# Second attention of a two-layer decoder: heads in pairs on the two halves of TensorE's rows

## The reference

```python
def _L1_attn_ref(x, W_qkv, b_qkv, W_proj, b_proj):
    B, N, C = x.shape                       # 2, 1024, 256
    qkv = x @ W_qkv + b_qkv
    qkv = qkv.reshape(B, N, 3, 16, 16)      # 16 heads of 16 columns
    q, k, v = jnp.transpose(qkv, (2, 0, 3, 1, 4))
    scores = jnp.einsum('bhqd,bhkd->bhqk', q, k) * 16 ** (-0.5)
    attn = jax.nn.softmax(scores, axis=-1)
    out = jnp.einsum('bhqk,bhkd->bhqd', attn, v)
    return jnp.transpose(out, (0, 2, 1, 3)).reshape(B, N, C) @ W_proj + b_proj
```

## Time and profile before

| | us |
|---|---|
| median of 3 runs | 2764.35 (2764.23 to 2765.06) |
| the profiled execution, own time | 2767.74 |
| its span in the trace | 2765.9 |
| second attention's loop | from 1894.0 to 2441.0 of the span |
| busy over the whole span | PE 91%, DVE 62%, ACT 46%, POOL 31% |

### The profile page before, as it was taken

The page is one execution under the profiler, slowest core; times in us unless marked ns, Lnnn a source line. Parts: engine busy times, 40 slices in busy tenths (PEclk is TensorE's granted clock), DMA queues, the critical chain, the costliest instruction groups (busy, mean ns, idle before and its releaser), DMA issues.

```text
span 2765.9 us, 35667 instructions
## 1 busy us (share of the span) xinstructions
PE 2511.4 (91%) x13840; PEld 1727.1 (62%) x13840; DVE 1717.4 (62%) x3089; ACT 1282.2 (46%) x2015; POOL 867.3 (31%) x445
## 2 busy tenths in 40 slices
PE   8999998999999789899999999997999999976663
PEld 7554545744554579788888988994555555544421
DVE  5566655376665446875444344356877777847967
ACT  4555554345555144344444444442666555632342
POOL 4777774366777240102222023010200000004323
PEclk9999999999999899899999999998999999987885
DMA  2000001000000210000000010003333232210000
GB/s 74 12 22 14 12 12 43 12 12 23 12 19 1 69 61 1 31 1 31 31 31 20 12 43 9 1 1 83 74 66 70 62 66 62 47 32 9 1 0 31
DMA packets 49641, 84.23 MB, mean 30 GB/s; under 512 B 9912, under 2 KB 30016, under 8 KB 49472
## 3 DMA queue, kind: packets, MB, share of 16 engines
q1 hardware_dynamic: 49328, 81.88, 11.6%
q10 hardware_dynamic: 144, 0.07, 0.0%
HBM read 37.49 MB, written 2.10 MB: 14 GB/s over the span
## 4 chain that ended last, share of the span: by engine, by line
PE 75%; DVE 16%; ACT 3%; issue 3%; POOL 2%; DMA 1%; SPq 0%; ACTq 0%; DVEq 0%; POOLq 0%
PE PS L85 74%; DVE m_gl L1097 2%; DVE PS L576 2%; DVE a_QS L554 1%; ACT a_P L519 1%; DVE a_nm L568 1%; DVE s_nm L1523 1%; DVE X L271 1%; DVE x_E L1922 1%; DVE x_rd L1906 1%; DVE st_s L232 1%; DVE x_sm L1927 1%; POOL f_H L2128 1%; POOL a_sum L676 1%; ACT a_QS L473 1%
## 5 line engine op out<-in xcount | busy, mean ns | idle before, releaser
L1097 DVE TENSOR_TENSOR m_gl<-m_g,m_gh 128x512 fp32r<-128x512 f32 x288 | 258.1, 902 | 386.4 <-ACT m_g L936 386.4
L676 POOL TENSOR_TENSOR a_sum<-a_sum,a_P 128x1024 f32<-128x1024 f32 x192 | 456.6, 2378 | 128.4 <-ACT a_P L519 118.0
L519 ACT ACTIVATE a_P<-PS 128x512 f32<-128x512 f32 x512 | 290.3, 596 | 354.3 <-PE PS L85 349.5
L933 ACT ACTIVATE m_gh<-PS,cols 128x512 fp32r<-128x512 f32 x288 | 198.5, 689 | 469.6 <-PE PS L85 469.6
L1523 DVE TENSOR_REDUCE s_nm<-PS 128x1 f32<-128x512 f32 x512 | 344.8, 688 | 70.0 <-PE PS L85 67.4
L568 DVE TENSOR_REDUCE a_nm<-PS 128x1 f32<-128x1024 f32 x256 | 300.4, 1216 | 128.2 <-PE PS L85 128.2
L85 PE MATMUL PS<-m_w2h,m_gh 128*128 128x256 f32 x1152 | 324.5, 282 | 18.9 <-DVE m_gl L1097 18.7
L1440 ACT ACTIVATE s_P<-PS 128x1024 f32<-128x1024 f32 x256 | 262.1, 1024 | 165.4 <-PE PS L85 164.8
L85 PE MATMUL PS<-m_w2l,m_gh 128*128 128x256 f32 x1152 | 323.1, 280 | 0.0
L85 PE MATMUL PS<-m_w2h,m_gl 128*128 128x256 f32 x1152 | 323.0, 280 | 0.0
L85 PE MATMUL PS<-a_P,a_V 128*64 128x512 f32 x1024 | 250.9, 612 | 0.0
(11 more groups left out here) (304 smaller groups left out, 4346.8 us busy)
## 6 DMA issues: line engine op xcount, KB each, us to landing
m_raw<-in_m_w SPq DMA_DIRECT2D x16, 1024.0 KB, 5.2
s_Q<-s_T SPq DMA_DIRECT2D x128, 128.0 KB, 2.4
s_K<-s_T SPq DMA_DIRECT2D x128, 128.0 KB, 2.4
a_KH<-a_KH SPq DMA_DIRECT2D x64, 128.0 KB, 2.3
a_wr<-in_w_qk SPq DMA_DIRECT2D x16, 256.0 KB, 2.9
X<-in_x SPq DMA_DIRECT2D x4, 512.0 KB, 6.6
a_P<-in_w_v SPq DMA_DIRECT2D x8, 256.0 KB, 5.8
a_P<-in_w_o SPq DMA_DIRECT2D x2, 1024.0 KB, 5.5
```

Source lines behind the costliest of these rows:

```text
L519: e.activation(a_P[:, g % N_P, half * 512:half * 512 + 512], PS[:, 2 + half, :], ACT.Exp).then_inc(s["a_exp"], 1)
L676: e.tensor_tensor(o[:, :], a_P[:, (g - 1) % N_P, :] if k == 1 else o[:, :], a_P[:, g % N_P, :], ALU.add).then_inc(s["a_add"], 1)
L933: e.activation(m_gh[r][:, :], PS[:, 4 + n % 3, :], func, bias=cols[:, bcol:bcol + 1]).then_inc(s["m_gh"], 1)
L1097: e.tensor_tensor(m_gl[r][:, :], m_g0[r][:, :], m_gh[r][:, :].bitcast(F32), ALU.subtract).then_inc(s["m_gl"], 1)
```

## The change

Heads go in pairs (`p`, 16 of them; two halves `q` of 512 queries in each). Each head of a pair has 64 partitions of `s_Q` and `s_K` (`R[0]` and `R[1]`): 32 for high times high with the maximum's row, 16 for low times high, 16 for high times low. Low times low is left out, and so is the maximum's low part (`s_ml`), since a shift that is the same everywhere cancels in the softmax. `R_S` is 3. There are 256 steps again, with as many matmuls of each kind; each of the natural and transposed ones now contracts over 64 partitions.

- natural: 128 queries by 512 keys of both heads, into bank pair 0, 1 or 2, 3; one DVE reduce over 1024 columns a step.
- transposed: 128 keys by 512 queries of both heads, head a into bank 4 + a. Each has its own exponential of 512 columns; the next matmul into that bank waits for it.
- values: two steps' worth together, in every second step. Bank 6 is copied once, by ACT, into `s_zt`, and SP moves it to `s_Z` with two DMAs.
- the gather is 12 DMAs for each pair, issued at step 16k + 15; the maxima's row goes in two DMAs for each half pair.
- `turned` for the first four tiles moves into the loop, the first projections use four banks, and transposed matmuls stand at a step's start.

```diff
-        R_S = 4
+        R_S = 3
-        s_P = [sb(c, f"s_P{i}", [128, S]) for i in range(3)]
+        s_P = [sb(c, f"s_P{i}", [128, S]) for i in range(4)]
+            if x in (228, 236, 244, 252):
+                side[x].append(("turned", (x - 228) // 8))
...
             for x in range(N_X):
-                if x < 8 * NH:
-                    natural(x, 0)
-                extra = list(side[x])
-                if extra and extra[0][0] == "rows":
-                    piece(extra.pop(0))
                 w = x - LAG_S
-                if 0 <= w < 8 * NH:
-                    h, kt = divmod(w, 8)
-                    bk = (2, 4)[w % 2]
+                if 0 <= w < N_U:
+                    p, half, kt = w // 16, (w // 8) % 2, w % 8
                     if kt == 0:
-                        e.wait_ge(s[f"row{h % 2}"], 256 + 32 * (h // 2 + 1))
-                    if w >= 2:
-                        e.wait_ge(s["s_exp"], w - 1)
-                    for half in range(2):
-                        t = mm(e, PS[:, bk + half, :], Ks[h % R_S][:, kt * 128:(kt + 1) * 128],
-                               Qs[h % R_S][:, half * 512:half * 512 + 512], True, True)
-                    t.then_inc(s["s_st"], 1)
-                if x < 8 * NH:
-                    natural(x, 1)
+                        e.wait_ge(s[f"row{(w // 8) % 2}"], 256 + 32 * (w // 16 + 1))
+                    for a in range(2):
+                        if w:
+                            e.wait_ge(s["s_exp"], 2 * w + a - 1)
...
+                        mm(e, PS[:, 4 + a, :], Ks[p % R_S][R[a], kt * 128:(kt + 1) * 128],
+                           Qs[p % R_S][R[a], half * 512:half * 512 + 512], True, True).then_inc(s["s_st"], 1)
+                if x < N_U:
+                    p, i, half = x // 16, (x // 2) % 8, x % 2
...
+                    for a in range(2):
+                        t = mm(e, PS[:, 2 * half + a, :], Qs[p % R_S][R[a], i * 128:(i + 1) * 128],
+                               Ks[p % R_S][R[a], half * 512:half * 512 + 512], True, True)
+                    t.then_inc(s["s_n"], 1)
                 y = x - LAG_P
-                if 0 <= y < 8 * NH:
...
+                if y % 2 and 0 < y < N_U:
+                    for y in (y - 1, y):
...
+                        for c in range(4):
+                            part = 512 * (c % 2) + 256 * (c // 2)
+                            t = mm(e, PS[32 * c:32 * c + 32, 6, 0:256], V1[:, kt, (h + c % 2) % 16, :],
+                                   s_P[y % 4][:, part:part + 256], kt == 0, kt == 7)
...
-                    e.activation(s_P[w % 3][:, :].rearrange("p (a n) -> p a n", a=2), PS[:, bk:bk + 2, :],
-                                 ACT.Exp, scale=0.25).then_inc(s["s_exp"], 1)
+                    for a in range(2):
+                        e.wait_ge(s["s_st"], 2 * w + a + 1)
+                        e.activation(s_P[w % 4][:, a * 512:a * 512 + 512], PS[:, 4 + a, :],
+                                     ACT.Exp, scale=0.25).then_inc(s["s_exp"], 1)
...
+                    e.tensor_reduce(nm2[:, p % 2, :, i, half], PS[:, 2 * half:2 * half + 2, :], AX.X, ALU.max,
+                                    negate=True).then_inc(s["s_nr"], 1)
...
         def sp_l1a(e):
-            def gather(h):
+            def gather(p):
+                g = p // 2
...
+                    e.wait_ge(s["s_b7"], n_b7["proj", g, 3])
+                if p >= R_S:
+                    e.wait_ge(s["s_st"], 32 * (p - R_S) + 32)
...
+                for what in side[x]:
+                    if what[0] == "rows":
...
+                        e.wait_ge(s["s_mhd"], q + 1)
...
-                if 0 <= w < 8 * NH and w % 8 == 7 and w // 8 + R_S < NH:
-                    gather(w // 8 + R_S)
+                if x >= 15 and x % 16 == 15 and x // 16 + 2 < N_PR:
+                    gather(x // 16 + 2)
```

More of the change, by code:

```diff
@@ L1227, in program @@
         for x in range(N_X):
-            if 0 <= x - LAG_M < 8 * NH and (x - LAG_M) % 8 == 0:
-                side[x].append(("rows", (x - LAG_M) // 8))
+            if x >= 9 and (x - 9) % 8 == 0 and (x - 9) // 8 < 2 * N_PR:
+                side[x].append(("rows", (x - 9) // 8))
             y = x - LAG_P
-            if 0 <= y < 8 * NH:
-                if y // 8 == 15:
-                    side[x].append(("values", y % 8))
-                if y % 32 == 31:
-                    pb, pg = y // 128, (y // 32) % 4
-                    todo += [("sums", pb, pg), ("spread", pb, pg), ("scale", pb, pg, 0), ("scale", pb, pg, 1)]
-                    if pg == 3:
-                        for q in range(2):
-                            todo += [("project", 8 * pb + j) for j in range(4 * q, 4 * q + 4)]
-                            todo.append(("norm", 8 * pb + 4 * q))
@@ L1241, in program @@
-            if todo and x // 8 % 4 > 1 and x % 8 in (3, 5, 7):
+            if y % 2 == 1 and 120 <= y < 128:
+                side[x] += [("values", y - 121), ("values", y - 120)]
+            if 0 <= y < N_U and y % 32 == 31:
+                pb, pg = y // 128, (y // 32) % 4
+                todo += [("sums", pb, pg), ("spread", pb, pg), ("scale", pb, pg, 0), ("scale", pb, pg, 1)]
+                if pg == 3:
+                    for q in range(2):
+                        todo += [("project", 8 * pb + j) for j in range(4 * q, 4 * q + 4)]
+                        todo.append(("norm", 8 * pb + 4 * q))
@@ L1251, in program @@
-        before = {7: len(i7), 6: None}
-        for i, what in enumerate(rest):
-            if what[0] not in ("spread", "norm"):
-                bank7[what], i7_free[what] = 7 - i % 2, before[7 - i % 2]
-                i7[what] = before[7 - i % 2] = len(i7) + 1
+                who = {"rows": "s_mhd", "turned": "t_xl"}.get(what[0], "s_b7")
+                count[who] += 1
+                i7_free[what], bank7[what], n_b7[what] = last_b7[bk], bk, count[who]
+                if what[0] != "turned":
+                    i7[what] = len(i7) + 1
@@ L1449, in act_l1a @@
-                for what in extra:
-                    if what[0] == "spread":
+                    if q >= 2:
+                        e.wait_ge(s[f"s_zd{q % 2}"], 32 * (q // 2))
+                    e.activation(s_zt[:, q % 2, :], PS[:, 6, 0:256], ACT.Copy).then_inc(s["s_za"], 1)
+                for what in side[x]:
+                    if what[0] == "rows":
+                        q = what[1]
+                        e.wait_ge(s["s_p7"], i7[what])
+                        if q >= 2:
+                            e.wait_ge(s[f"row{q % 2}"], 256 + 32 * (q // 2))
+                        e.activation(s_mh[:, q % 2, :], PS[0:8, 7, 0:128], ACT.Copy).then_inc(s["s_mhd"], 1)
+                    elif what[0] == "spread":
@@ L1533, in piece @@
                     tiles = range(what[1], what[1] + 4)
-                    slow.append(norm_steps(e, own, tiles, {j: (s["s_b7"], i7["project", j]) for j in tiles}))
+                    slow.append(norm_steps(e, own, tiles, {j: (s["s_b7"], n_b7["project", j]) for j in tiles}))
+                elif what[0] == "turned":
+                    late.append(what)
                 elif what[0] == "proj":
                     late.append(what)
-                elif what[0] != "spread":
+                elif what[0] not in ("spread", "rows"):
                     bk = bank7[what]
@@ L1559, in dve_l1a @@
                     slow.append(round_steps(e, own, range(6)))
-                if x < 8 * NH:
-                    natural(x, 0)
-                if late:
-                    _, g, u = late.pop()
-                    low(g, u, 7).then_inc(s["s_b7"], 1)
-                extra = list(side[x])
-                if extra and extra[0][0] == "rows":
-                    _, h = extra.pop(0)
-                    e.wait_ge(s["s_mhd"], h + 1)
-                    e.tensor_tensor(s_ml[:, h % 2, :], PS[0:8, 7, 0:128], s_mh[:, h % 2, :].bitcast(F32),
-                                    ALU.subtract).then_inc(s["s_b7"], 1)
@@ L1589, in dve_l1a @@
             pump(slow, 99)
-            for i in range(4):
-                turned(i, i % 2)
             for what in rest:
```

278 lines of the change are left out of this document (125 added, 153 removed).

## The result

The changed kernel takes 2794.6 us as a median of four runs (2788.3 to 2800.5). The kernel before took 2764.3 beside it, so the ratio is 1.0111, with an interval of [1.0088, 1.0134]: 1.1% slower, some 30 us. The forecast was 2771.

A forecast was written before the change was run, and what follows sets the result against it. PE was taken to bound the loop, busy 499.4 of 505.4 us. Pairs and pieces -20, SP queue +25, loop's end +4, behind the loop -2 sum to +7: 2774.7 profiled, 2771 as median; range 2736 to 2798.

The forecast's parts named there:

- The sign: Whole kernel: slower than before, sum +7 us; chance of slower 0.46, same 0.17, faster 0.37.
- Rival 3: PE's score matmuls: none run side by side, natural pair adds 0.23 in the step with values; 2790 us; chance 0.15.
- Rival 4: PE's clock falls: a fifth of the loop at half clock costs some 40 us; 2810 us; chance 0.08.
- -20 + 25 = +5: The loop: -20 us from bare pairs and pieces together, +25 from late DMAs in the SP queue.
- The bare pair: Two steps without pieces: 3.34 us against 3.40, a chain through both exponentials; 121.5 pairs give -7 us.
- Side by side: Both heads' matmuls on different array rows run at once, rather than one after the other at 0.23 us each.
- The SP queue: The 12-DMA gather delays the maxima's row behind it, so transposed matmuls wait: 23 plus 2, +25 us.
- Rival 1: SP queue: the rows' DMAs are in time, so the +25 us goes; 2746 us; chance 0.22.
- The clock: PE's granted clock: a fall to half speed was left out of the sum and held only as a rival, 0.08.
- The pieces: Extra work between steps partly fills PE's idle time: rows -9, `scale` -7, `sums` -4, `project` -4, `turned` +3, projections +7.5 us.
- Rival 2: PE or exponentials run tighter: pair at 3.1 or less, 2742 us, far end 2667; chance 0.15.
- Start, end, tail: Loop's start 0, its end without natural matmuls +4 us at 3.11 a pair, behind the loop -1.9 us.

The follow-up runs named there:

- e6: e1 with both heads' score matmuls on the same upper half of the array's rows, the second head's own scores left out: 2886.2 us, ratio 1.0461.
- e1: The changed kernel with the 12-DMA gather issued behind the maxima's row of step 16k+17 instead of ahead of it: 2758.2 us, ratio 0.9978.
- e12: e7 with the gather put back ahead of the maxima's row in SyncE's queue, as in the changed kernel: 2759.9 us, ratio 0.9983.
- e7: e2 with each step's eight values matmuls in that step again, not two steps' together: 2706.7 us, ratio 0.9792.
- e4: The kernel before the change with only the values' matmuls of two steps put together behind every second step: 2761.5 us, ratio 1.0003.
- e9: e7 with each `sums` piece cut in two, four weight loads behind one step and four behind the next: 2700.2 us, ratio 0.9772.
- e2: e1 with the second head's transposed matmul moved behind the natural pair within a step: 2737.3 us, ratio 0.9905.

## Why the prediction came out as it did

The sign and both main mechanisms were right, the size was 24 us short. 2794.6 lies near the upper end of the stated range, 2736 to 2798, but above the 2758 to 2784 over which the forecast's own 0.40 was spread: that the range held it is owed in good part to the room left for rivals 3 and 4. Step by step, for the loop, where the forecast was -20 + 25 = +5 and 30.9 was measured:

- **The bare pair.** Predicted 3.34, measured 3.40. The chain is the predicted one, link by link: two exponentials 1.08 for 1.09, 0.05 for 0.06 to the next matmul, 0.67 for 0.66 to the values, 1.00 behind them. The link that was off most is the first: the scores are with ACT after 0.60 (2150.82 to 2151.42), I had 0.53, the figure of a single matmul behind values. 0.06 x 121.5 = 7. The pair gained nothing over 2 x 1.70.
- **Side by side.** Right, by the trace (the natural pair 0.34 behind the transposed one, its two matmuls 0.01 apart) and by e6. Rival 3 falls.
- **The SP queue.** Predicted 25, measured 26.2 in 13 stops, at the matmul and for the DMA that the text named; e1 removed it and e12 moved it by the amount that the counting gives. Rival 1 falls. The sum agrees better than its parts: 11 stops were counted for 13, the first cost 1.7 for 3.7, and the others 0.4 to 3.4; that is luck. Without this step the change is a small gain (e1), with it a loss.
- **The clock.** This is the step that failed. I had it as a rival with 0.08 that excluded the forecast, and put nothing of it into the sum. It came in part with the stops: 86 us at half clock in the changed loop, for under 2 before. Twelve falls lie in it: six in or behind a stop (34 us), five behind `sums`, some with a stop inside (37 us), and one at the end (7 us); 11 us more are left over at its start. 56 of the 86 go with e1 and cost 12.5; the other 30, most of them behind `sums` and at the ends, cost 7 more at the same rate, an estimate. Rival 4 said 40 for a fifth of the loop at half clock; it was a sixth, and 19 us, since PE, as I take it, waits for ACT during more than a quarter of it anyway (0.9 of the 3.40).
- **The pieces.** The rest of the -20 was -13. With the pair at 3.40 and 7 for the clock, e1's loop should be -20 + 7 + 7 = -6 us from the one before; it is -7.8. The pairs of steps of both traces say the same: 25 bare ones at full clock are 3.45 on the average in both kernels, 85 with pieces together 17 us shorter, 11 that are at half clock in either 10 longer. The kinds are off, partly against each other: a pair with a projection grew by 0.16 (0.3 was put down), those with `sums`, `project` and `scale` shrank by 1.0, 0.8 and 0.7 (0.5, 0.5 and 0.55). So the pieces' sum holds within 4 us, and of the 30.9: 5 forecast, 7 pair, 1 waits, 19 clock, and -1 left over.
- **Start, end, tail.** What lies behind the loop is 0.6 longer; I had +4 and -1.9. A pair without natural matmuls takes 3.16 (2447.90 to 2451.05) for 3.11.
- **Rival 2** was false for the change as written, but its chain can be shortened: with the row ahead of the gather, the natural pair ahead of the second wait and values in every step, the pair is 2.72 and the kernel takes 2707, 2.1% less than before. Its far end, 2667, was not reached. The Trainium skill's page "TensorEngine Tiling (Array Packing)", section "PSUM Bottleneck", says that packing speeds up TensorE and not the emptying of PSUM. The trace agrees as long as the order puts both exponentials into the chain (135.1 us of PE's waits); in e7 these waits are 74.9.

Open stays what the chip reacts to when the clock falls with PE busy in the records. Nearly all of these falls came within 3 us behind a `sums` piece, though not every such piece was followed by one. The kernel before, with the same pieces in its loop, had none; but e4, whose scores' matmuls fill all rows as well, had one, so these falls are not confined to the kernels with half-filled rows. e9 thinned them out. I did not try a `sums` piece of the same length with other shapes. Nor did a run undo the other parts of the change by themselves: the copy through `s_zt`, three operand buffers for four, `turned` in the loop.

## What to carry to other kernels

When a change makes a burst in a DMA queue longer, count the issues (0.63 us each here) from what releases the burst to the small, urgent transfer behind it, and set them against the steps until its need: the small one goes first, and the shorter the steps get, the more it matters (26 us of stops, 46 with shorter steps). A buffer of its own for each half of a result is worth only as much as the queue can do while the second half is still being emptied: the same edit was worth 0 in one arrangement and 97 us in another, so look at the order before judging the part. Where an engine gains idle time, book the clock too: by the reckoning above, 86 us at half clock cost 19 us here.

## What the runs showed of the hardware that I had not expected

- The granted clock fell to half, and stayed there, with PE's records busy throughout (e6: busy for all 7 us from 2083 to 2090 at 1.00, then 48 of 48 us at 0.50), so the busy share of the profile does not forecast it.
- Matmuls on the two halves of the array's rows need not be neighbours of one kind, and they need not start in the queue's order. In e2 the queue has the first head's transposed matmul, then the first and the second head's natural ones. The trace starts the transposed one at 2099.04, the second head's natural one (known by the semaphore that it raises) at 2099.05 and the first head's at 2099.38; it is so in 241 of the loop's 243 natural pairs, and in the changed kernel in one.
- An exponential starts 0.60 behind the start of such a pair, for 0.53 behind a single full-array matmul.
